# Layer 1's three bf16 parts summed in PSUM, layer 0's weights formed in the matching stage, and 256 weight additions ahead of the experts

## What is computed

```python
def gcn_conv(x, src, dst, W, b, n):
    h = x @ W
    deg = jnp.zeros((n,), h.dtype).at[dst].add(1.0)
    dinv = jax.lax.rsqrt(jnp.maximum(deg, 1e-12))
    norm = dinv[src] * dinv[dst]
    msg = h[src] * norm[:, None]
    return jax.ops.segment_sum(msg, dst, num_segments=n) + b
h = jax.nn.relu(gcn_conv(x, src, dst, W1, b1, n))
z = jax.nn.relu(gcn_conv(h, src, dst, W2, b2, n))
h = jax.nn.relu(gcn_conv(z, src, dst, W3, b3, n))
x_hat = gcn_conv(h, src, dst, W4, b4, n)
```

## Time and profile before

| | us |
|---|---|
| median of 3 runs | 3905.28 (3905.13 to 3913.46) |
| profiled execution | 3902.96 |
| its span | 3901.2 |
| PE busy | 2937.5 (75%) |
| DVE busy | 1776.3 (46%) |
| ACT busy | 922.0 (24%) |
| POOL busy | 2365.0 (61%) |
| POOL, 391 count additions (L504), busy | 659.4, mean 1.686 each |
| POOL, 391 weight additions (L1263), busy | 637.6, mean 1.631 each |

### The profile page before, as it was taken

How to read it: one execution, slowest core, us unless ns; L and a number is a source line. 1 busy time by engine, 2 the same in 40 slices (tenths; PEclk the granted TensorE clock), 3 DMA queues, 4 the chain that set the end, 5 groups by cost and what they waited for, 6 DMA issues and landing times.

```text
span 3901.2 us, 47597 instructions
## 1 busy us (share of the span) xinstructions
PE 2937.5 (75%) x15015; PEld 2144.8 (55%) x15016; DVE 1776.3 (46%) x4716; ACT 922.0 (24%) x2170; POOL 2365.0 (61%) x1883
## 2 busy tenths in 40 slices
PE   2999753787868957890899989989987545456798
PEld 2566541564566557880788877855444333234565
DVE  4778458355776851106312122234434444344344
ACT  1555322135555412332201000022110000001121
POOL 7888788886888887778565566500032666662121
PEclk9999966788999958995899999989988776675799
DMA  8445522226576557774435533301225333336232
GB/s 308 104 121 121 106 1 0 12 9 171 132 163 139 122 123 193 211 215 91 124 119 205 183 100 117 117 32 53 79 91 163 93 94 91 91 93 154 82 126 77
DMA packets 295154, 451.34 MB, mean 116 GB/s; under 512 B 166999, under 2 KB 223103, under 8 KB 281332
## 3 DMA queue, kind: packets, MB, share of 16 engines
q1 hardware_dynamic: 129232, 295.34, 24.1%
q0 software_dynamic: 161232, 108.44, 17.2%
q10 hardware_dynamic: 4464, 44.80, 2.8%
HBM read 320.02 MB, written 127.88 MB: 115 GB/s over the span
## 4 chain that ended last, share of the span: by engine, by line
PE 41%; DVE 17%; another core or an unknown queue 7%; issue 5%; DVEq 3%; DMA 2%; ACT 1%; SPq 1%; POOL 0%; ACTq 0%; POOLq 0%
PE g_acc L2356 12%; PE f2m_pR L3079 4%; DVE X L1355 3%; PE g3g_pp L1326 3%; PE f2m_pR L3051 3%; PE f3e_pH L3514 3%; PE f1e_pH L2800 3%; PE f3e_pY L3523 3%; PE f1e_pY L2823 2%; PE f2m_pO L3062 1%; DVE g3g_hot L1333 1%; PE g_acc L1867 1%; PE g_psL L2340 1%; DVE sort_run L2209 1%
## 5 line engine op out<-in xcount | busy, mean ns | idle before, releaser
L504 POOL DMA_INDIRECT count_cells<-cells_count,added_row x391 | 659.4, 1686 | 130.4 <-issue 114.6
L1263 POOL DMA_INDIRECT weight_cells<-added_weight,added_row x391 | 637.6, 1631 | 142.1 <-issue 113.8
L2356 PE MATMUL g_acc<-g_H,g_blocks 125*125 125x256 f32 x2500 | 572.7, 386 | 22.7 <-issue 11.4
L2258 POOL DMA_INDIRECT slots_dram<-sort_rec,sort_row x392 | 380.2, 970 | 279.4 <-issue 123.2
L1313 POOL DMA_INDIRECT g3a_got<-relations,g3g_idx x388 | 378.9, 977 | 270.4 <-PE g3g_pp L1326 112.6
L2356 PEld LDWEIGHTS g_acc<-g_H,g_blocks 125*125 125x125 f32 x2500 | 472.2, 191 | 104.8 <-issue 33.9
L1326 PE MATMUL g3g_pp<-g3a_got,g3g_hot 128*125 128x256 f32 x840 | 302.3, 510 | 273.9 <-DVE X L1355 156.5
L1326 PEld LDWEIGHTS g3g_pp<-g3a_got,g3g_hot 128*125 128x125 f32 x840 | 192.8, 249 | 383.8 <-issue 353.8
L1355 DVE TENSOR_TENSOR X<-X,g3g_pp 125x256 f32 x420 | 176.8, 421 | 325.9 <-remote 181.3
L2423 DVE SCALAR_TENSOR_TENSOR g_tmp<-g_acc,dinv,g_b 125x256 f32<-125x256 f32 x50 | 24.2, 484 | 490.3 <-PE g_acc L2356 248.0
L1948 ACT CAST g_blocks<-g_blocks 128x3125 f16<-128x3125 uint16 x85 | 236.6, 2793 | 40.9 <-DMA g_blocks<-count_cells 40.1
(11 more groups left out here) (760 smaller groups left out, 5421.3 us busy)
## 6 DMA issues: line engine op xcount, KB each, us to landing
g_blocks<-weight_cells SPq DMA_DIRECT2D x49, 1562.5 KB
g_blocks<-count_cells SPq DMA_DIRECT2D x85, 781.2 KB, 10.8
weight_cells<-edges_stripe ACTq DMA_DIRECT2D x25, 1562.5 KB
f1e_w<-in_L_ffn_w SPq DMA_DIRECT2D x68, 512.0 KB
relations<-f2m_ys SPq DMA_DIRECT2D x25, 896.0 KB
f_w<-in_L_ffn_w SPq DMA_DIRECT2D x16, 1024.0 KB
count_cells<-edges_XT POOLq DMA_DIRECT2D x19, 781.2 KB
relations<-zeros SPq DMA_DIRECT2D x10, 1000.0 KB
```

The lines of the kernel that those rows point to most:

```text
L504: pool.indirect_dma_start(out=rows, out_offset=bass.IndirectOffsetOnAxis(ap=g.cell_row[:, t:t + 1], axis=0), in_=g.cell_count[:, t:t + 1], ...
L1263: pool.indirect_dma_start(out=rows, out_offset=bass.IndirectOffsetOnAxis(ap=g.cell_row[:, t:t + 1], axis=0), in_=g.cell_weight[:, t:t + 1] ...
L2258: pool.indirect_dma_start(out=g.slots_dram[:, :], out_offset=bass.IndirectOffsetOnAxis(ap=self.row[:, c:c + 1], axis=0), in_=self.rec[:, c ...
L2356: last = nc.tensor.matmul(acc[0:P, i % 3, 0:D], blocks[0:P, i % BLOCKS, t * P:(t + 1) * P], H[p][0:P, t, :], start=(t == 0), stop=(t == T ...
```

## The change

Three things are changed.

- Layer 1: each matmul of 3 x WIDTH columns becomes three matmuls of WIDTH columns into the same columns of PSUM, which accumulate (75 in place of 25 for each block, each with its own load of the weights), and the same for the heavy correction (3 in place of 1). The sum of the three parts is then complete in PSUM, and `take` reads it once: pass 0 has one multiply-add, pass 1 has one multiply-add ahead of the relu and the split, passes 2 and 3 have one copy.
- Layer 0: the separate stage that loads x and forms the weights is removed. SP loads the weights and attention vectors ahead of the matching's own loads, DVE forms the two products after step n = 2 of the matching, x is loaded in the stage of the degrees, and DVE's wait for the zero fills goes to the end of that stage.
- `BEFORE_EXPERTS` goes from 284 to 256, so that 28 weight additions move from before the experts' loop to behind it (59 become 87).

```diff
-BEFORE_EXPERTS = 284
+BEFORE_EXPERTS = 256
...
-def cells_and_degrees(nc, g, e):
+def cells_and_degrees(nc, g, e, first_load, prepare, next_load):
...
             @block.sync
             def _(sp):
+                first_load(sp)
                 same.load(sp)
...
                     for norm in norms:
                         norm.step(dve, n)
+                    if n == 2:
+                        prepare(dve)
...
         with stage(nc, g) as block:
+            @block.sync
+            def _(sp):
+                next_load(sp)
+
             @block.tensor
...
                 g.heavy.number(dve, pdeg)
+                dve.wait_ge(g.counts_filled, 16 * ACT_FILLS)
+                dve.wait_ge(g.counts_filled_too, 16 * (T - ACT_FILLS))
...
-        cells_and_degrees(nc, g, e)
-
-        with stage(nc, g) as block:
-            @block.sync
-            def _(sp):
-                for lo, hi in STRIPS:
-                    sp.dma_start(g.X[lo:hi], e.x_dram.rearrange("(p t) d -> p t d", p=P)[lo:hi]).then_inc(e.x_loaded, 16)
...
+        def attend(dve):
+            dve.wait_ge(w_loaded, 48)
+            for k, out in ((0, wl[:, :, :]), (1, w[:, :, D:D + 4])):
+                nc.vector.tensor_tensor(turned_att[:, :, :], w[:, :, 0:D], wide(att[:, k, :], 128, K2, D), ALU.mult)
+                dve.drain()
+                nc.vector.tensor_reduce(out, turned_att[:, :, :].rearrange("p k (h d) -> p k h d", h=4), AX, ALU.add)
+                dve.drain()
...
+        cells_and_degrees(nc, g, e, load_weights, attend, load_x)
...
                 for t in range(lo, hi):
-                    last = nc.tensor.matmul(acc[:, i % ACCS, 0:3 * WIDTH[p]], blocks[0:P, place(p, j), t * P:t * P + 128],
-                                            rhs[p][0:P, t, 0:3 * WIDTH[p]], start=(t == 0), stop=False)
+                    for k in range(3):
+                        last = nc.tensor.matmul(acc[:, i % ACCS, 0:WIDTH[p]], blocks[0:P, place(p, j), t * P:t * P + 128],
+                                                part(p, t, k), start=(t == 0 and k == 0), stop=False)
...
-                nc.tensor.matmul(acc[:, i % ACCS, 0:3 * WIDTH[p]], spread_rows[:, j, :], heavy_rows[:, 0:3 * WIDTH[p]],
-                                 start=False, stop=True).then_inc(summed, 1)
+                for k in range(3):
+                    last = nc.tensor.matmul(acc[:, i % ACCS, 0:WIDTH[p]], spread_rows[:, j, :],
+                                            heavy_rows[:, k * WIDTH[p]:(k + 1) * WIDTH[p]], start=False, stop=(k == 2))
+                last.then_inc(summed, 1)
...
-                sums = [acc[0:P, i % ACCS, k * w:(k + 1) * w] for k in range(3)]
+                whole = acc[0:P, i % ACCS, 0:w]
                 dve.wait_ge(summed, i + 1)
-                nc.vector.tensor_copy(some[0:P, 0:w], sums[2])
-                dve.drain()
-                nc.vector.tensor_tensor(some[0:P, 0:w], sums[1], some[0:P, 0:w], ALU.add)
-                dve.drain()
...
+                if p == 1:
+                    nc.vector.scalar_tensor_tensor(out=some[0:P, 0:w], in0=whole, scalar=dinv, in1=b2[0:P, :],
                                                    op0=ALU.mult, op1=ALU.add).then_inc(acc_read, 1)
...
+                if p == 0:
+                    nc.vector.scalar_tensor_tensor(out=u[0:P, m % 2, 0:w], in0=whole, scalar=dinv, in1=b1[0:P, :],
+                                                   op0=ALU.mult, op1=ALU.add).then_inc(acc_read, 1)
+                else:
+                    nc.vector.tensor_copy(u[0:P, m % 2, 0:w], whole).then_inc(acc_read, 1)
+                dve.drain().then_inc(u_ready, 1)
```

More of the change, by code:

```diff
@@ L1412, in layer0_gnn @@
         w_loaded = sem("w_loaded")
-        cells_and_degrees(nc, g, e)
-        with stage(nc, g) as block:
-            @block.sync
-            def _(sp):
-                for lo, hi in STRIPS:
-                    sp.dma_start(g.X[lo:hi], e.x_dram.rearrange("(p t) d -> p t d", p=P)[lo:hi]).then_inc(e.x_loaded, 16)
[L1421 to L1429, removed]
-                    dve.drain()
-                    nc.vector.tensor_reduce(out, turned_att[:, :, :].rearrange("p k (h d) -> p k h d", h=4), AX, ALU.add)
-                    dve.drain()
-                dve.wait_ge(g.counts_filled, 16 * ACT_FILLS)
-                dve.wait_ge(g.counts_filled_too, 16 * (T - ACT_FILLS))
@@ new lines, in load_weights @@
+        def load_weights(sp):
+            sp.dma_start(w[:, :, 0:D], a["L0_gnn_weight"].rearrange("(k p) n -> p k n", p=128)).then_inc(w_loaded, 16)
+            sp.dma_start(att[:, 0, :], a["L0_gnn_attn_l"].rearrange("h d -> (h d)").partition_broadcast(128)).then_inc(w_loaded, 16)
+            sp.dma_start(att[:, 1, :], a["L0_gnn_attn_r"].rearrange("h d -> (h d)").partition_broadcast(128)).then_inc(w_loaded, 16)
+        def attend(dve):
[5 more added lines that the diff above has]
+                dve.drain()
@@ L1436, in put, with load_x @@
+        def load_x(sp):
+            for lo, hi in STRIPS:
+                sp.dma_start(g.X[lo:hi], e.x_dram.rearrange("(p t) d -> p t d", p=P)[lo:hi]).then_inc(e.x_loaded, 16)
+        cells_and_degrees(nc, g, e, load_weights, attend, load_x)
         def put(dve, i, product, bias):
@@ L2021, in take @@
                     dve.drain()
+                    return
+                m = TURN[p] + j
+                if m >= 2:
+                    dve.wait_ge(turned, m - 1)
+                if p == 0:
[4 more added lines that the diff above has]
+                dve.drain().then_inc(u_ready, 1)
             def put(p, k):
```

## The result

| | before | changed |
|---|---|---|
| median, us | 3905.72 (3882.84 to 3922.14, 20 runs) | 3922.17 (3912.61 to 3930.75, 20 runs) |
| ratio | | 1.0043 (95%: 1.0030 to 1.0056) |
| profiled execution's span | 3901.2 | 3914.1 |
| PE busy | 2937.5 | 2947.1 |
| DVE busy | 1776.3 | 1706.4 |

The change makes the kernel slower by 0.43%, about 17 us; 3908 was predicted. The range of 3897 to 3930 holds the time, but its likeliest case, no change within 0.2%, did not come: the time lies on the slower side, near rival (c)'s 3918.

A forecast was written before the change was run, and what follows sets the result against it. No single limit; GpSimd's additions set layer 2's start, meeting layer 1's path at the experts. Added tail 51.4 minus layer 1's 49, layer 0 at 0, gave +2.4: forecast 3908 us, 8-in-10 range 3897 to 3930.

The forecast's parts named there:

- (c): Layer 1, passes 1 and 2: casts and transfers hold the period at 3.1 to 3.2; about 3918 us, chance 0.13.
- Part 1: GpSimd around the experts: 28 additions moved behind the loop lengthen the tail by 51.8, costing 51.4 at layer 2's start.
- The 10.8 of waits: GpSimd's last 28 additions before the experts: time above 51.8, expected to stay ahead of the experts.
- The 0.4 taken as hidden: Layer 2's start: 0.4 us of the longer tail hidden behind the Sync queue's own loads.
- Part 3: Layer 0's weights formed during matching: early loads and VectorE's products covered by GpSimd's lag, 0 us; 3 to 5 if uncovered.
- The prediction's own sign: Layer 1's start on TensorE should stay at about 890; the prediction is wrong if it moves.
- Part 2: Layer 1's split matmuls accumulating in the same columns: VectorE loses operations, making layer 1 49 us shorter.
- S: Time by which layer 1 gets shorter: 49 us, bounds 34 and 57, useful up to 52.9.
- (a): Layer 1, passes 1 and 2: small matmuls miss 29 ns, TensorE bounds from about 37; 3940 or 3980, chance 0.11.
- (b): Layer 1, all passes: load and matmul cost 80 ns whatever the columns; about +250 us, 4155, chance 0.04.
- (d): GpSimd's additions in layer 1 get cheaper and S is over 59; faster by 10 us, 3895, chance 0.10.

The follow-up runs named there:

- l1_284: Kernel before with only layer 1's matmul change, keeping 284 weight additions ahead of the experts: 3898.57 us, ratio 0.998.
- b256: Kernel before with only 256 in place of 284 weight additions ahead of the experts: 3912.0 against 3876.38 us, ratio 1.0098.
- l1_80: Changed kernel without the layer 0 change and with only 80 weight additions ahead of the experts: 4220.79 us, one run.
- l1_256: Changed kernel without the layer 0 change, with 256 additions ahead of the experts: 3904.29 us, ratio 0.9992; repeated 3904.38, ratio 1.0008.
- late_load: Changed kernel with layer 0's loads behind the matching's ninth window and products after step 20: 3878.93 against 3876.38 us, ratio 1.002.

## Why the prediction was right and wrong

**The bound** was read rightly. Two paths meet at the experts, and POOL sets layer 2's start: `l1_284` (54.65 us of idle PE, 0.2% of gain) and `b256` (68.94 us of idle POOL, 1% of loss) show both halves.

**Part 1** (28 additions): 51.8 predicted, 51.6 measured. The additions ahead of the experts: POOL was expected to be ready 1414.0 − 890.37 = 523.6 after layer 1's start, and was ready 1432.11 − 904.93 = 527.2 after it. The 10.8 of waits did stay in front. The 0.4 taken as hidden were 4.2: I took the landing as seen at 1891.75, where POOL saw it, but in the changed kernel the Sync queue asks for its blocks 5.21 after the last addition's start (1910.76), and in the one before 8.59 after it (1892.16), because its own loads stood in front. The last of them in the kernel before, right ahead of the 1892.16 of the earlier trace rows:

```profile
1891.58 0.47 SPq L2300 DMA_DIRECT2D g_columns<-in_L_gnn_ln_b  x1
```

The time to be read there was that of the queue's own work, not POOL's.

**Part 3** in the prediction's count (layer 0's weights) is the step that failed. "Both are covered as long as GpSimd is behind the windows it is given": it is, for all windows but the first; in the changed kernel the profile puts the wait of the first addition alone down to DVE. In the kernel before DVE hands over the first window at 89.92 and POOL, still busy with its gathers, takes it at 95.67: a cover of 5.7 us. These are the two rows that I should have set beside the loads:

```profile
89.92 0.16 DVE L1137 TENSOR_TENSOR added_row<-same_away,cells_trash 128x8 int32<-128x8 f32 x1
...
95.67 1.62 POOL L504 DMA_INDIRECT count_cells<-cells_count,added_row  x1 [0.30 <-issue]
```

and these are the answers of the changed kernel, with PE's first scores (71.04 before):

```profile
76.83 0.28 PE L1083 MATMUL same_scores<-edges_other,edges_own 11*128 11x128 bf16 x1 [13.71 <-DMA edges_other<-digits_dram]
...
99.87 0.16 DVE L1137 TENSOR_TENSOR added_row<-same_away,cells_trash 128x8 int32<-128x8 f32 x1
```

Three loads of 2.6 us of issuing make the digits land 5.8 later, the window is handed over 9.95 later, and 5.2 of that show in POOL. "If that cover is gone, it costs 3 to 5" was right for this wait alone; by the time it got to layer 1 it was 14.6 in this trace, and 12 in the time of the comparison on one chip. And since POOL is the bound up to layer 2, nothing there absorbs it. The prediction's own sign had come with that: it calls itself wrong if layer 1's start has moved, and it moved from 890 to 905. The gain of the removed stage went, as predicted, into PE's wait before layer 1, which is 52.82 in place of 11.92; 35 was predicted, and 14.6 of it is the later start.

**Part 2** (S): 49 predicted, 43 measured. Pass 0 and pass 3 were right within 1 us, and the two matmul rates were 55.9 and, in a block without a gap, 29.2 ns against 55.8 and 29.2. What was mis-sized are the terms of passes 1 and 2, 22 and 9 against 17.5 and 6.0. I let VectorE and the casts set the period and took it that blocks and products are there in time. They are not always: PE has 12.5 us of gaps of its own in the two passes, ACT waits for blocks, and the additions beside the passes cost a part, as `l1_80` shows, by a way that is open. The size is that of rival (c), for which I had S = 34 to 43 and about 3918.

**The rivals.** (a) came only in part: the small products run at the 29 ns that I took and, with the gaps on PE, at 33.9 in the block shown, under the 37 from which they decide. (b) falls: 55.9 ns for a 128-column product with its own load, in a stream of 75. The Trainium skill's 81 ns for a sustained stream at N = 128 ("TensorE: Matmul & The Clock Gate", "Back-to-back issue gap") isn't met here; the formula which that section calls the isolated gap is. (d) did not come. (c) gave 6 us of S and no more; that the time lies near its 3918 is luck. By the sum above, 14.6 in place of 0 for the loads and 6 for S, less the 3.8 hidden and the 1.4 of loop and tail, make up the error at layer 2. The range holds the time, but for the loads it had allowed only 3 to 5.

**Chances.** Slower by over 0.2% had 0.28, within 0.2% had 0.62. `l1_256`, the change without the step I priced at zero, has its median within 0.2% in both of its comparisons (0.9992 and 1.0008).

## What to carry to other kernels

When one engine has no idle time from its first instruction to the point that matters, price a moved load at the place where that engine is fed for the first time: its slack there is the whole cover, however far behind it is later. If two paths meet, shortening one and moving work off the other only help together, and work that is moved behind the meeting point comes back in full if the same engine sets the next one. An engine's idle slots are then the only thing to win: sixteen additions put into the experts' loop, at half price, were worth more than the 43 us taken from layer 1.

## What the hardware showed

- A stream of matmuls with their own 128-wide loads runs at 55.9 ns for 128 columns (75 in 4.19 us) and at 29.2 ns for 64 (75 in 2.19 us). In passes 1 and 2 the latter has short gaps on PE for which the profile names nothing, 12.5 us in 31 places; a block with one ran at 33.9 ns (75 in 2.54 us).
- The same indirect addition takes 1.85 us from start to start where it is undisturbed. Beside such additions VectorE's casts of 125x128 took 265 ns in place of 227, and two passes were 4.3 and 5.6 us longer in one pair of traces (78.3 to 74.0, 91.9 to 86.3).
- Three loads that take 2.6 us to issue, ahead of the matching's digits on one queue, made the digits land 5.8 us later (TensorE's first scores at 76.83 in place of 71.04, and at 71.19 in `late_load`, where they stand behind the ninth window).
